# A recommendation tower on one core: layer 2 in half groups with the dots stationary, gathers that wait for finished tiles, weights loaded in pieces

## What is computed

```python
e = stack([tbl_f[ids[:, f]] for f in range(39)])          # (512, 39, 16)
for W in (W0, W1):                                        # two layers
    xk = einsum('bid,bjd,ijh->bhd', e, xk, W.reshape(39, Hk, 128))
    outs.append(xk)                                       # Hk: 39, then 128
z = sum(concatenate(outs, axis=1), axis=-1)               # (512, 256)
h = relu(concatenate([z, dense_ctx], 1) @ W_top1 + b_top1)   # 272 -> 512
h = relu(h @ W_top2 + b_top2)                                # 512 -> 256
y = h @ W_top3                                               # 256 -> 1
```

## Time and profile before

| | us |
|---|---|
| median of 3 runs | 255.88 (254.53 to 257.08) |
| the profiled execution | 256.75 |
| its span, first to last instruction | 254.9 |
| TensorE busy | 206.8 (81%) |
| VectorE busy | 180.5 (71%) |
| GpSimd busy | 156.8 (61%) |
| ScalarE busy | 149.4 (59%) |
| mean granted clock of TensorE | 0.96 |

### The profile page before, as it was taken

How to read it: one execution, slowest core, us unless ns; L and a number is a source line. 1 busy time by engine, 2 the same in 40 slices (tenths; PEclk the granted TensorE clock), 3 DMA queues, 4 the chain that set the end, 5 groups by cost and what they waited for, 6 DMA issues and landing times.

```text
span 254.9 us, 3934 instructions
## 1 busy us (share of the span) xinstructions
PE 206.8 (81%) x1198; PEld 164.2 (64%) x1212; DVE 180.5 (71%) x335; ACT 149.4 (59%) x284; POOL 156.8 (61%) x165
## 2 busy tenths in 40 slices
PE   0378384770988898999897979998989799998996
PEld 0123242550756586888685868886758688877995
DVE  1487495953999979797979697979796968841000
ACT  2034345570878776677686666776875566865002
POOL 4877777777777777777777777777777750000000
PEclk9999979796799999999999999999999799999799
DMA  6300023297321202121202120202021201010000
GB/s 176 86 6 6 6 32 90 34 241 177 86 44 22 32 10 29 12 30 12 31 9 31 12 28 10 35 7 35 6 31 10 32 7 19 6 30 1 0 3 0
DMA packets 27511, 9.40 MB, mean 37 GB/s; under 512 B 22513, under 2 KB 25585, under 8 KB 27490
## 3 DMA queue, kind: packets, MB, share of 16 engines
q1 hardware_dynamic: 22370, 7.86, 14.0%
q0 software_dynamic: 5120, 1.29, 6.0%
HBM read 6.50 MB, written 0.00 MB: 26 GB/s over the span
## 4 chain that ended last, share of the span: by engine, by line
POOL 45%; PE 24%; issue 17%; DMA 6%; DVE 5%; ACT 2%; POOLq 0%; DVEq 0%; ACTq 0%
POOL gathered L346 45%; PE tower L669 7%; DMA gathered<-table,rows 5%; PE copies L620 3%; PE ring L658 2%; PE ring L659 1%; PE ring L660 1%; PE sums L634 1%; PE sums L636 1%; DVE turned L406 1%; PE sums L635 1%; DVE prod L418 1%; DMA ids_sb<-ids 1%; ACT dots L530 1%; ACT prod_hi L496 1%
## 5 line engine op out<-in xcount | busy, mean ns | idle before, releaser
L346 POOL DMA_INDIRECT gathered<-table,rows x160 | 156.4, 978 | 51.0 <-issue 46.3
L426 DVE TENSOR_TENSOR prod_lo<-prod,prod_hi 128x512 fp32r<-128x512 f32 x96 | 64.9, 689 | 2.2 <-ACT prod_hi L496 2.1
L418 DVE TENSOR_TENSOR prod<-first,copies 128x512 f32<-128x512 f32 x96 | 64.0, 681 | 2.0 <-ACT first L487 1.3
L496 ACT CAST prod_hi<-prod 128x512 fp32r<-128x512 f32 x96 | 58.3, 625 | 8.9 <-DVE prod L418 7.6
L620 PE MATMUL copies<-turned,sel_sb 128*128 128x512 bf16 x98 | 38.1, 433 | 29.0 <-DVE turned L406 28.7
L669 PE MATMUL tower<-dots,w_sb 128*128 128x128 f32 x312 | 49.8, 284 | 2.7 <-DVE turned L406 2.3
L669 PEld LDWEIGHTS tower<-dots,w_sb 128*128 128x128 f32 x312 | 47.6, 199 | 5.0 <-issue 1.1
L634 PE MATMUL sums<-prod_hi,w_hi 128*128 128x512 f32 x96 | 47.4, 494 | 0.1
L530 ACT COPY dots<-ring 128x320 f32<-128x320 f32 x64 | 43.6, 748 | 6.3 <-PE ring L660 5.7
L620 PEld LDWEIGHTS copies<-turned,sel_sb 128*128 128x128 bf16 x112 | 10.2, 102 | 44.0 <-DVE turned L406 34.1
L636 PE MATMUL sums<-prod_hi,w_lo 128*128 128x512 f32 x96 | 38.4, 400 | 0.0
(11 more groups left out here) (85 smaller groups left out, 237.1 us busy)
## 6 DMA issues: line engine op xcount, KB each, us to landing
gathered<-table,rows POOLq DMA_INDIRECT x160
diag<-columns SPq DMA_DIRECT2D x128, 20.0 KB
wt_sb<-wt SPq DMA_DIRECT2D x2, 512.0 KB
sel_f<-sel SPq DMA_DIRECT2D x1, 448.0 KB, 3.2
w0a<-w_ij SPq DMA_DIRECT2D x1, 448.0 KB, 4.8
w0b<-w_ji SPq DMA_DIRECT2D x1, 448.0 KB, 6.3
ids_sb<-ids SPq DMA_DIRECT2D x1, 85.0 KB, 2.0
ident_f<-ident SPq DMA_DIRECT2D x1, 64.0 KB, 3.3
```

The costliest lines, as they stand in the source:

```text
L346: pool.indirect_dma_start(gathered[0:n, k % NGATHER, q, :], None, table, bass.IndirectOffsetOnAxis(ap=rows[0:n, k, q:q + 1], axis=0)).then ...
L418: nc.vector.tensor_tensor(prod[:, m % NPROD, :], first[:, k % 2, :], copies[n % 3][:], ALU.mult)\
L426: nc.vector.tensor_tensor(prod_lo[:, m % NPART, :], prod[:, m % NPROD, :], prod_hi[:, m % NPART, :], ALU.subtract).then_inc(lo_ready, 1)
L496: nc.scalar.copy(prod_hi[:, m % NPART, :], prod[:, m % NPROD, :]).then_inc(hi_ready, 1)
```

## The change

Layer 2 is done per half group (64 samples, two blocks). The operands change places: a field's dots (128 x 64) are stationary and W1's slice (128 x 128) moves. Even fields write partitions 0 to 63 of the bank, odd fields 64 to 127, so a result is in two parts with samples on the partitions. ScalarE copies both (`part`), and one matmul with two stacked 64 x 64 identities (`fold`) adds them and turns them back into `z2`. The tower still runs per group, now three steps. W1 is laid out by field, loaded in 13 pieces of three fields, each after one product of the first blocks; the other weights follow in pieces. A gather waits for the tile that lies 23 gathers behind.

```diff
+HALF_TENSOR = dict(layer2=6.2, rate=6.5, fold=13.4)
+HALF_SCALAR = dict(part=13.0, z2=14.4)
+TOWER_TENSOR = (15.6, 29.2, 32.2)
+TOWER_SCALAR = (19.0, 31.6, 33.6)
+TOWER_VECTOR = 17.0
...
+    for half in range(HALVES - 1):
+        end = STEPS * (HALF // BLOCK) * (half + 1)
+        pe.extend((end + HALF_TENSOR["layer2"] + i / HALF_TENSOR["rate"], ("layer2", half, i)) for i in range(FIELDS))
+        pe.append((end + HALF_TENSOR["fold"], ("fold", half)))
...
+            def load_w1(n):
+                sp.dma_start(w1_sb[:, THIRD * n:THIRD * n + THIRD, :], w1[:, THIRD * n:THIRD * n + THIRD, :]).then_inc(w1_in, 16)
...
             def load_weights(k):
+
+                for t in range(TILES):
+                    n = TILES * k + t
+                    sp.wait_ge(prod_ready, n + 1)
+                    if n < FIELDS // THIRD:
+                        load_w1(n)
+                    elif t in (1, 2):
+                        load_wt1(t - 1)
+                    elif t in (3, 4):
+                        load_wt2(t - 3)
+                    else:
+                        sp.dma_start(wt3_sb[:], wt3).then_inc(tower_in, 16)
+                        sp.dma_start(bt2_sb[:], bt2).then_inc(tower_in, 16)
...
                 for q in range(QUARTER):
-                    if k >= 2 and q % 2 == 0:
-
-                        pool.wait_ge(prod_ready, TILES * (k - 2) + q // 2 + 1)
+                    m = QUARTER * k + q
+                    if m >= AHEAD:
+
+                        pool.wait_ge(tile_used, TILES * (m - AHEAD) // QUARTER + 1)
...
+            def store_part(half):
+                act.wait_ge(part_full, half + 1)
+                if half:
+                    act.wait_ge(fold_full, half)
+                nc.scalar.copy(part[:], tower[:, 0:P]).then_inc(part_stored, 1)
...
-            def second_layer(g, i):
+            def second_layer(half, i):
+                g, at = divmod(half * HALF, GROUP)
...
-                mm = pe.matmul(tower[:, 0:GROUP], w1_sb[:, i, :], dots[:, g % 2, i, :],
-                               start=(i == 0), stop=(i == FIELDS - 1))
+                side = HALF * (i % 2)
+                mm = pe.matmul(tower[side:side + HALF, 0:P], dots[:, g % 2, i, at:at + HALF], w1_sb[:, i, :],
+                               start=(i < 2), stop=(i >= FIELDS - 2))
                 if i == FIELDS - 1:
-                    mm.then_inc(tower_full, 1)
+                    mm.then_inc(part_full, 1)
+
+            def fold(half):
+
+                pe.wait_ge(part_stored, half + 1)
+                pe.matmul(tower[:, P:P + HALF], part[:], ident_f[:, P:P + HALF], start=True, stop=True).then_inc(fold_full, 1)
...
+            for i in range(FIELDS):
+                second_layer(HALVES - 1, i)
             last_first_layer(0)
             last_first_layer(1)
-            for i in range(FIELDS):
-                second_layer(GROUPS - 1, i)
+            fold(HALVES - 1)
             last_first_layer(2)
             last_first_layer(3)
```

More of the change, by code:

```diff
@@ L142, in orders @@
                     items.extend((STEPS * k + step, (name, k, n)) for n, step in enumerate(steps))
[L143 to L149, removed]
+    for half in range(HALVES - 1):
+        end = STEPS * (HALF // BLOCK) * (half + 1)
+        pe.extend((end + HALF_TENSOR["layer2"] + i / HALF_TENSOR["rate"], ("layer2", half, i)) for i in range(FIELDS))
+        pe.append((end + HALF_TENSOR["fold"], ("fold", half)))
+        act.extend((end + step, (name, half)) for name, step in HALF_SCALAR.items())
+        if half % 2:
+            pe.extend((end + step, ("tower", half // 2, n)) for n, step in enumerate(TOWER_TENSOR))
+            act.extend((end + step, ("tower", half // 2, n)) for n, step in enumerate(TOWER_SCALAR))
+            dve.append((end + TOWER_VECTOR, ("h1", half // 2)))
     return [[what for _, what in sorted(items, key=lambda x: x[0])] for items in (pe, act, dve)]
@@ L211, in build @@
         bt2_sb = sb("bt2_sb", [P, H2 // P])
+        part = sb("part", [P, P])
         z2 = sb("z2", [P, GROUP])
@@ L532, in store_dots, with store_z2 @@
                     .then_inc(ring_drained, 1)
+            def store_part(half):
[3 more added lines that the diff above has]
+                nc.scalar.copy(part[:], tower[:, 0:P]).then_inc(part_stored, 1)
+            def store_z2(half):
+                g, at = divmod(half * HALF, GROUP)
+                act.wait_ge(fold_full, half + 1)
+                if g:
+                    act.wait_ge(tower_full, NMLP * (g - 1) + 1)
+                nc.scalar.copy(z2[:, at:at + HALF], tower[:, P:P + HALF]).then_inc(z2_stored, 1)
             def tower_step(g, step):
-                act.wait_ge(tower_full, NMLP * g + step + 1)
                 if step == 0:
-                    last = nc.scalar.copy(z2[:], tower[:, 0:GROUP])
+                    act.wait_ge(h1_summed, g + 1)
+                    nc.scalar.activation(h1[:], h1[:], ACT.Relu).then_inc(h1_ready, 1)
                 if step == 1:
-                    act.wait_ge(h1_summed, g + 1)
-                    last = nc.scalar.activation(h1[:], h1[:], ACT.Relu)
-                if step == 2:
+                    act.wait_ge(tower_full, NMLP * g + 2)
                     for n in range(H2 // P):
@@ L544, in tower_step @@
                                                     bias=bt2_sb[:, n:n + 1])
-                if step == 3:
-                    last = nc.scalar.copy(y[:, GROUP * g:GROUP * g + GROUP], tower[0:1, 0:GROUP])
-                last.then_inc(tower_drained, 1)
+                    last.then_inc(h2_ready, 1)
+                if step == 2:
+                    act.wait_ge(tower_full, NMLP * g + 3)
+                    nc.scalar.copy(y[:, GROUP * g:GROUP * g + GROUP], tower[0:1, 0:GROUP]).then_inc(y_stored, 1)
             def store_dense():
@@ L560, in _ @@
                  "high": high, "squares": square_both, "sums": store_x1, "x1": store_turned,
-                 "dot": store_dots, "tower": tower_step}[what[0]](*what[1:])
-            tower_step(GROUPS - 1, 0)
+                 "dot": store_dots, "part": store_part, "z2": store_z2, "tower": tower_step}[what[0]](*what[1:])
+            store_part(HALVES - 1)
+            store_z2(HALVES - 1)
             for n in range(H1 // P):
@@ L683, in tower_step @@
                         mm = pe.matmul(to, wt1_sb[:, 1, cols], z2[:], start=False, stop=True)
-                if step == 2:
+                if step == 1:
+                    pe.wait_ge(z2_stored, 2 * g + 3)
+                    pe.wait_ge(h1_ready, g + 1)
                     for n in range(H2 // P):
@@ L688, in tower_step @@
                                            h1[:, j, :], start=(j == 0), stop=(j == H1 // P - 1))
[L689 removed]
+                if step == 2:
+                    pe.wait_ge(h2_ready, g + 1)
                     for j in range(H2 // P):
@@ L707, in _ @@
                      "tile": add_tile, "sum_squares": add_squares, "x1": turn_x1, "dot": dot,
-                     "layer2": second_layer, "tower": tower_step}[what[0]](*what[1:])
+                     "layer2": second_layer, "fold": fold, "tower": tower_step}[what[0]](*what[1:])
             pe.wait_ge(prod_ready, TILES * BLOCKS)
```

82 lines of the change are left out of this document (44 added, 38 removed).

## The result

The changed kernel took 282.83 us (median of four runs, 282.09 to 284.38) beside 256.48 us (254.53 to 257.38) of the kernel before on the same chip: 1.105 times as long, with an interval of 1.099 to 1.110. The forecast was slower, 276.1 us in a range of 253 to 292. The sign and the cause hold; the size was 6.7 us too small. Later the same program was run on another chip and was faster than the kernel before; that is told with the experiments, since it decides which of them can be read against this result.

The account below looks back on a forecast made before the run. Gathers bound the kernel before, TensorE the changed one: block 3 at 58.9, list 197.2, waits 1.5, half clock 1 give 258.6; the end's 16.5 makes 275.1, forecast as 276.1 us after correction to the runs' median, range 253 to 292.

Parts of the forecast that it names:

- Gathers set the pace before; TensorE after: Main list: GpSimd's gathers set 12.5 us a block before; the change makes TensorE set 14.4 us a block.
- The price of a change of shape: Layer 2 on TensorE: each run pays 0.34 us to enter and leave the 64-wide form; 89 runs, 30.3 us.
- Rival A: Layer 2's changes of form cost nothing, gathers bound again, 252.8 us or 251; chance 0.15.
- What n matmuls cost: Layer 2: a run of n matmuls takes n + 1 slots of 0.1115 us, since the two column halves overlap.
- Rival B: Layer 2's two column halves do not overlap, 20.5 us more in the list and 4.2 at the end: 299.8; chance 0.15.
- Where block 3 starts: With weights loaded in pieces, block 3 is turned at 58.9 us, 4 us earlier, starting the long TensorE stretch.
- 1.5 us of waits: TensorE's waits from block 3 to the last dot: 1.5 us, taken over from the old list.
- The half clock: TensorE right after the wait at 59 us runs at half clock, costing about 1 us.
- The reckoning: Last dot: 58.9 for block 3, 197.2 of TensorE's list, 1.5 of waits, about 1 of half clock: 258.6 us.
- The end: After the last dot: the last half of layer 2 gets shorter, giving back 3.8 us, 16.5 instead of 20.3.
- Pacing and pieces at nothing: Gathers waiting for tiles cost nothing; weights in pieces cost nothing beyond bringing block 3 4 us earlier.
- The signs that were named: Next profile: TensorE busy over 90%, last gather past 225 us, run of six 0.8 plus 0.34, last 39 about 4.5.

Follow-up runs that it names:

- The last experiment: Changed kernel with each half group's layer 2 in one run and ScalarE's relu behind the dots: 253.25 us, 0.989 of the kernel before.

## Why the prediction was right, and what it missed

**Gathers set the pace before; TensorE after.** Right: 14.6 us a block instead of 12.5 (predicted 14.4).

**The price of a change of shape.** Right, and it carries the result: 0.34 taken from the two odd places of the earlier trace rows, 0.33 measured, 89 times. Rival A (nothing) is out. The last experiment's kernel shows that the cost goes with the number of runs, and the one with the weights stationary that it goes with the shape: the same runs, 1.35 us for six matmuls whose instructions take 1.34. The Trainium skill ("TensorEngine Tiling (Array Packing)", Key Properties) has the drain at a change of tiling mode; the late weight load of L675 above agrees (0.00 us ahead of its matmul, where that of L676 is 0.23 ahead). One reading of the prediction was too sharp: the load at 247.91 in the earlier trace rows does not begin when the matmul before has run out, but 0.08 us ahead of its modelled end.

**What n matmuls cost.** Nearly right. The halves overlap in full, but from pair to pair the stream does not slide: an odd matmul pays for a whole pair. A run takes 2 x ceil(n/2) slots, not n + 1: 320 slots in the list instead of 362. With 0.33 for 0.34, 5.6 us less than forecast. Rival B (no overlap) is out: 4.48 us from the first start of the last half to the next instruction where 8.7 would be without overlap and 4.46 was forecast. The page that spoke for B (the Trainium skill, "TensorE: Matmul & The Clock Gate", Part 3: a weight load overlaps only where the row group differs) is contradicted by this trace, if that sentence is taken alone: every matmul of layer 2 uses all 128 rows, and they overlap. The same part also lets a load into the background weight buffer run ahead of running matmuls, which fits.

**Where block 3 starts.** Turned at 59.91 against 58.9: its last gather took 3.88 us to land, not 2.2, though it was issued 0.6 us earlier. Right within 1.0.

**1.5 us of waits: the step that failed.** I carried the waits of the old list over to the new one. The new list has its own: three times 2.12 us behind the relu, 1.40 before the last dots, 1.02 and 0.62 elsewhere, 9.4 us in all, 10.4 with the 0.17 us by which the next start lies further off than the idle time says. The prediction priced the tower's steps on TensorE but never laid ScalarE's and VectorE's order beside them. That the relu causes the stalls is shown by the kernel with it moved by 1.2 steps, where the last tower's dot no longer waits, and by the last experiment, where none of the three is left. What they cost alone, some 6 to 7 us, is read from the trace and was not measured where before takes 256 us.

**The half clock.** About 1 us was allowed. The two windows above are granted 0.87 on average, so 3.4 of 13 us at the lower level (1.2 of 2.4 GHz), which costs up to 1.7 in each: one after the wait for block 3, one after the stall at 121 us. The other two stalls of that length cost no clock (granted 1.00 in their stretches). So 3.4 us.

**The reckoning.** 59.9 + (197.2 - 5.6) + 10.4 + 3.4 = 265.3; the last dot ended at 265.25. The terms of the forecast were 58.9 + 197.2 + 1.5 + 1.0 = 258.6. The stretches at the lower clock may hold a little of the stalls, so the sum is good to a microsecond, not to the tenth.

**The end.** 15.05 us for 16.5: the last half as forecast, and the half clock that I left in (0.13 of 13 us, 1.7) is gone, since TensorE ran at a granted clock of 1.00 from 265 us on. The 0.2 us that are left the other way are not traced.

**Pacing and pieces at nothing.** Right on chips of the first kind: 1.0005 (0.997 to 1.004). Wrong on the others, where tile waits are the gain. The prediction had no row from which that could be seen.

**The signs that were named.** TensorE busy over 90%: 86% of the span, but 207.4 of the 221.0 us from 59 to 280. Last gather past 225 us: 223.4. A run of six at 0.8 and 0.34 us: 1.00 in all. The last 78 instructions at about 4.5: 4.48.

## What to carry to other kernels

Before a matmul is cut into narrower tiles to be spread between other work, count the runs and not the matmuls: each run pays its way in and out, here 0.33 us, as much as three 128-column instructions of 0.1115. Keep such tiles in one long run per batch, and in even numbers. When an order of work is rewritten, read the in-order neighbours on every engine that frees a buffer: an instruction that waits for a slower engine holds back the copy behind it. And time a change on more than one chip if its gain lies in waits.

## What the hardware showed that I had not expected

- One program, two rankings: 1.105 of the kernel before where that takes 256 us, 0.965 where it takes 327. Three chips were of the second kind (327 to 333 us before) and two of the first (254 and 256), beside that of the result. Why some handovers are late there, the longest seen by 8 us, stays open; instruction times at the same clock and the landing of gathers hardly differ, and the recorded semaphore updates do (2393 against 6201).
- Two 64-column matmuls of f32 in different halves of the array cost one (4.48 us for 78 instructions; 8.25 us when neighbours share a half, 8.73 us at full width).
- With all 128 columns of the array an f32 instruction stays at 0.112 us even when only 64 columns move (78 in 8.73 us).
